# Routing of a mixture of experts moved from between the attention's units to behind its last one

## The chip, the cores and the metric

The kernel runs on one core of a Trainium2 chip. The metric is the device time of one execution in microseconds (us). The core has five engines with a queue each: TensorE (PE), VectorE (DVE), ScalarE (ACT), GpSimd (POOL) and SyncE (SP), which here only issues DMAs. Engines wait for each other by semaphores. A program part that is written as one block ends with a barrier of all five engines: none starts on the next block before each has come to the end of its own queue.

## The reference

`x` is 8 batches of 512 tokens with 128 channels. Four layers are added to it in turn, each on the layer-normalized input:

```
x = x + power_attention(layernorm(x))   # 16 heads of 8, (q.k)^2 with a decay
x = x + ffn(layernorm(x))               # 8 experts, top 1
x = x + delta_rule(layernorm(x))
x = x + ffn(layernorm(x))               # the same weights
```

The expert layer, which the change touches, is

```
logits = (x @ w_red) @ (wg / |wg|).T          # 8 experts
gates  = softmax(logits); idx = argmax(gates)
y      = gelu(x @ w1[idx] + b1[idx]) @ w2[idx] + b2[idx]
out    = y * gates[idx]
```

## The kernel before

The program is four blocks: `attention`, `experts` (f=0), `delta_rule`, `experts` (f=1).

**Attention.** A batch is 24 units (`NU`), each a strip of the causal score matrix. All loops are unrolled in Python, and each engine has its own function `batch(b, k)` that loops over units `n` and fixes the order of its queue by hand: numbers such as `TURN`, `QK`, `VALUES`, `SUMS`, `FIN` and the `R_...` constants say behind which unit a piece of other work stands. For a unit PE makes scores (`scores`, L1154) two units ahead, DVE takes their magnitude (`magnitude`, L795, one `a_mag` instruction a unit, also two ahead), ACT squares it (L552), POOL multiplies the diagonal blocks by a decay (`diagonal`, L415), and PE multiplies by the values (`attend`, L1183 and L1186) one unit later. Between them stands the preparation of the next batch: `a_xn` (L715) is DVE's behind unit 5 and `a_tail` (L773) behind unit 18, and POOL's `values_off` (L363) from unit 21 into unit 3 of the next batch. Behind units 2 and 20 the halves of a batch are finished (`turn_back` on PE, `finish` on DVE, `add_half` on POOL).

**Routing before.** While batch b runs, batch b-1 is routed for the first expert layer: `r_moments`, `r_deviation`, `r_normalize` on DVE, `r_turn` and `r_logits` on PE, `r_choose` on DVE, `r_ranks` on PE, `r_place` on DVE, all between units 8 and 19, and four `r_scatter` on POOL, each an indirect DMA of 128 rows of `r_xa` into `xs_dram`, at the expert's place that `r_place` found. In the last batch these stand two units earlier, with four more scatters. The gate's weights are made in batch 0 (`r_weights`, `r_gate`, `gate_turned`, `gate_weight`). Batch 7 alone is left to the `experts` block, which then makes the tables of tiles (`tables`), fills the expert areas' ends with blank rows (8 DMAs of `blank`, on ACT's queue) and loads on SP the weights and rows of the first slots.

**Experts.** 24 tiles of 256 rows go through slots of four: PE turns the rows (`turn_x`), multiplies by w1 (`up`, L1792) and w2 (`down`), turns back; POOL scatters the result. The order on PE is turn of the next slot, then `up` of this one. In the second `experts` block (f=1) all 8 batches are routed in five groups, `GROUPS` = (0), (1), (2,3), (4,5), (6,7).

Of the kernel before, what the change touches and what calls it, by code (L numbers as in the profile page):

```python
# [13 lines left out]
P = 128  # L14
# [24 lines left out]
ST = 256  # L39
# [7 lines left out]
SINGLE = tuple((b, b + 1) for b in range(B))  # L47
# [12 lines left out]
def attention(nc, x, xin, W, xs_dram, fs, keep, w_red, wg, b1, b2):  # L60
    with ExitStack() as ctx:
# [61 lines left out]
        r_stats = sb("r_stats", [P, TT, 6])  # L123
        r_mv = sb("r_mv", [P, TT, 2])
        r_rstd = sb("r_rstd", [P, 4, TT])
        r_xa = sb("r_xa", [P, 2, TT, C + 1])
        r_T = sb("r_T", [P, T])
        r_top = sb("r_top", [P, TT])
        r_hit = sb("r_hit", [P, TT, E])
        r_first = sb("r_first", [P, TT])  # L130
        r_oh = sb("r_oh", [P, TT, E], BF16)
        r_at = sb("r_at", [P, TT, E])
        r_pos_f = sb("r_pos_f", [P, TT])
        r_pos = sb("r_pos", [P, 2, TT], I32)
# [4 lines left out]
        b_in = sb("b_in", [E * NF + E, P])  # L139
        before, ones_r, one_row, pref, area = (keep[n] for n in ("before", "ones", "one_row", "pref", "area"))  # L140
        lgx, cnt, w_gate, blank = (keep[n] for n in ("lgx", "cnt", "w_gate", "blank"))
# [52 lines left out]
        def r_scat(c):  # L194
            return (fs["scat_done"], fs["scat_odd"])[c % 2]

        def r_logit_bank():
            return M1[:, 0:E * TT].rearrange("p (i e) -> p i e", e=E)

        def r_rank_bank(lo, hi):  # L200
            return M1[:, 64 + E * lo:64 + E * hi].rearrange("p (i e) -> p i e", e=E)
# [10 lines left out]
        def _(sp):  # L212
# [54 lines left out]
            for b in range(1, B - 2, 2):  # L267
                batch(b, 1)
                batch(b + 1, 0)

        @block.gpsimd
        def _(pool):
# [52 lines left out]
            def const(ins):  # L325
# [24 lines left out]
                      allow_small_or_imprecise_dtypes=True).then_inc(fs["f_consts"], 1)  # L350

# [66 lines left out]
            def r_index(c):  # L418

                if c >= 2:  # L420
                    pool.wait_ge(r_scat(c), 16 * TT * (c // 2))
                pool.iota(r_xa[:, c % 2, :, C], [[P, TT]], base=T * c, channel_multiplier=1,
                          allow_small_or_imprecise_dtypes=True).then_inc(fs["id_done"], 1)

            def r_scatter(c, i):
                pool.wait_ge(fs["pos_done"], c + 1)
                pool.wait_ge(fs["id_done"], c + 1)
                pool.indirect_dma_start(xs_dram[:, :], bass.IndirectOffsetOnAxis(ap=r_pos[:, c % 2, i:i + 1], axis=0),
                                        r_xa[:, c % 2, i, :], None).then_inc(r_scat(c), 16)
# [7 lines left out]
            def batch(b, k, first=False, last=False):  # L437
                for n in range(NU):
# [9 lines left out]
                    if n in R_SCATTER and b >= 2:  # L448
                        r_scatter(b - 2, R_SCATTER.index(n))
                    if n == R_SCALE2 + 1 and not first:  # L450
                        r_index(b - 1)
                    if last:
                        if n in R_SCATTER_LAST:
                            r_scatter(b - 1, R_SCATTER_LAST.index(n))
                        continue
# [17 lines left out]
        def _(act):  # L473
# [103 lines left out]
            def batch(b, k, first=False, last=False):  # L577
                for n in range(NU):
# [19 lines left out]
                    if last:  # L598
                        continue
# [2120 lines left out]
```

## Time and profile before

| | us |
|---|---|
| median of 3 runs | 1153.15 |
| lowest, highest | 1153.13, 1154.1 |
| the profiled execution | 1146.83 |
| its span, first to last instruction | 1145.0 |
| PE, DVE, ACT, POOL busy in it | 851.1, 760.2, 535.8, 562.0 |

The profiled execution was 6.3 us shorter than the median. Times in the rows count from the start of its span. Stretches are cut where the magnitude of a unit starts on DVE: 82.00 is unit 0 of batch 1 (`batch` starts anew with a 1024-column magnitude behind `a_rnorm`), 55.32 unit 8 of batch 0, 75.17 unit 20, and so on for the others.

### The profile page before, as it was taken

To read this page: it belongs to the slowest core of one execution; us is meant where nothing else is said; L and a number is where in the kernel's file an instruction comes from. 1 tells how busy PE (TensorE), PEld (TensorE's weight loads), DVE (VectorE), ACT (ScalarE), POOL (GpSimd) and SP (SyncE) were. 2 spreads that over 40 slices of the span, in tenths; PEclk is the share of its full clock that TensorE was granted. 3 is DMA by queue.
4 is the path that set the end of the run, shared out by engine and by line. 5 is a ranking of instruction groups with operands and counts; after the bars stand their busy time and mean duration, and the time that the engine had idled before them with its cause. 6 is when DMAs were issued, how large, how long until landed. Compare 5 with 4: busy or idle time off the path is not lost. (4 is left out here: it accounts for less than half of the span.)

```text
span 1145.0 us, 26725 instructions
## 1 busy us (share of the span) xinstructions
PE 851.1 (74%) x9326; PEld 632.7 (55%) x9326; DVE 760.2 (66%) x1722; ACT 535.8 (47%) x1219; POOL 562.0 (49%) x698
## 2 busy tenths in 40 slices
PE   3678888888888753999188999467867674629992
PEld 2455555555555542888124786156655563528881
DVE  7577687786877741223364889999999997512224
ACT  4577667586675721454055220255555531115450
POOL 4456557575665631445550010277777841533442
PEclk9998888797887965999688999878889886559996
DMA  5342241432414004566338400000020110155665
GB/s 162 112 157 91 68 159 41 134 98 70 159 41 134 9 14 139 168 202 187 100 58 109 74 1 0 0 1 0 0 73 0 37 38 7 40 157 163 196 195 165
DMA packets 129207, 101.80 MB, mean 89 GB/s; under 512 B 20640, under 2 KB 116832, under 8 KB 129056
## 3 DMA queue, kind: packets, MB, share of 16 engines
q1 hardware_dynamic: 120080, 87.27, 27.6%
q0 software_dynamic: 5120, 10.53, 2.6%
q10 hardware_dynamic: 3904, 2.61, 0.7%
q8 instruction: 68, 1.11, 0.4%
q14 instruction: 35, 0.29, 0.1%
HBM read 57.98 MB, written 35.45 MB: 82 GB/s over the span
## 5 line engine op out<-in xcount | busy, mean ns | idle before, releaser
L795 DVE TENSOR_SCALAR a_mag<-a_pS 128x1024 int32<-128x1024 int32 (+1 forms) x192 | 179.9, 949 | 66.6 <-PE a_pS L1154 65.7
L552 ACT ACTIVATE a_pw<-a_mag,a_eps_a 128x1024 f32<-128x1024 f32 (+1 forms) x192 | 175.0, 936 | 56.7 <-DVE a_mag L795 50.7
L1438 POOL DMA_INDIRECT ys_dram<-f_yo,f_who x96 | 92.1, 960 | 133.6 <-DVE f_yo L1703 116.9
L415 POOL TENSOR_TENSOR a_pw<-a_pw,a_decay 128x256 f32<-128x256 f32 x128 | 93.4, 730 | 105.2 <-ACT a_pw L552 104.5
L1154 PE MATMUL a_pS<-a_qf,a_kf 64*64 64x192 bf16 (+3 forms) x1536 | 112.2, 272 | 5.2 <-DVE a_mag L795 4.5
L1513 ACT ACTIVATE f_hs<-f_bH,f_bs 128x256 f32<-128x256 f32 x192 | 75.4, 475 | 69.0 <-PE f_bH L1792 69.0
L2613 PE MATMUL d_c<-d_pb_p,ident 128*128 128x256 f32 x256 | 72.3, 452 | 42.1 <-POOL d_pb_p L2096 42.1
L1186 PE MATMUL a_pOff<-a_pw,a_vo 128*18 128x64 f32 x3584 | 95.9, 241 | 1.2 <-issue 1.2
L1792 PE MATMUL f_bH<-f_xsT,f_w1s 128*128 128x256 f32 x384 | 95.6, 394 | 0.0
L1688 DVE TENSOR_SCALAR f_ysT<-f_bY,f_bs 128x256 f32<-128x256 f32 x48 | 23.2, 483 | 108.2 <-PE f_bY L1802 108.2
L1802 PE MATMUL f_bY<-f_hs,f_w2s 128*128 128x256 f32 x384 | 90.8, 379 | 0.0
L2613 PEld LDWEIGHTS d_c<-d_pb_p,ident 128*128 128x128 f32 x256 | 58.5, 232 | 56.3 <-issue 40.8
L1154 PEld LDWEIGHTS a_pS<-a_qf,a_kf 64*64 64x64 bf16 x1536 | 65.8, 116 | 30.7 <-DVE a_mag L795 7.6
L2613 PE MATMUL d_c<-d_pb_d,ident 128*128 128x256 f32 (+1 forms) x256 | 64.6, 419 | 21.7 <-POOL d_pb_d L2096 21.7
L2090 POOL TENSOR_TENSOR d_pb_p<-d_Q,d_s_sb 128x512 f32<-128x512 f32 x32 | 37.5, 1171 | 83.1 <-ACT d_s_sb L2198 83.1
L1186 PEld LDWEIGHTS a_pOff<-a_pw,a_vo 128*18 128x18 f32 x3584 | 68.6, 110 | 15.9 <-issue 11.4
L1792 PEld LDWEIGHTS f_bH<-f_xsT,f_w1s 128*128 128x128 f32 x384 | 72.4, 199 | 8.9
L1802 PEld LDWEIGHTS f_bY<-f_hs,f_w2s 128*128 128x128 f32 x384 | 69.4, 190 | 7.5
L2613 PEld LDWEIGHTS d_c<-d_pb_d,ident 128*128 128x128 f32 x256 | 53.1, 220 | 33.1 <-POOL d_pb_d L2096 24.6
L363 POOL TENSOR_TENSOR a_vo<-a_vd,a_reach 128x1008 f32<-128x1008 f32 (+6 forms) x56 | 66.0, 1194 | 1.1 <-issue 1.1
L1703 DVE COPY f_yo<-f_bO 128x256 f32<-128x256 f32 x48 | 20.4, 425 | 62.0 <-PE f_bO L1813 62.0
L2194 ACT ACTIVATE d_G<-d_c,d_g_ahead 128x64 f32<-128x64 f32 x64 | 24.1, 376 | 71.2 <-DVE d_og L2431 71.2
(395 smaller groups left out, 1837.9 us busy)
## 6 DMA issues: line engine op xcount, KB each, us to landing
parts_scratch<-a_parts SPq DMA_DIRECT2D x32, 384.0 KB, 3.4
f_w1s<-in_L_ffn_w_dram SPq DMA_DIRECT2D x48, 256.0 KB
f_w2s<-in_L_ffn_w_dram SPq DMA_DIRECT2D x48, 256.0 KB
a_kf<-parts_scratch SPq DMA_DIRECT2D x16, 512.0 KB, 4.8
a_qf<-parts_scratch SPq DMA_DIRECT2D x16, 512.0 KB, 5.6
f_xs<-xs_dram SPq DMA_DIRECT2D x48, 129.0 KB, 2.3
parts_scratch<-a_parts SPq DMA_DIRECT2D x16, 256.0 KB, 2.4
xs_dram<-blank ACTq DMA_DIRECT2D x16, 129.0 KB, 4.2
```

What stands on the lines that cost most here:

```text
L363: pool.tensor_tensor(vo[:, vo_at(j, j + 1):vo_at(j, j + 1) + n, :, :], vd[:, k, j, :, :].unsqueeze(1).broadcast_to([P, n, NP, 18]), reach[ ...
L415: pool.tensor_tensor(own, own, decay[:, k, m, hf:NP:2, :], ALU.mult)\
L552: act.activation(pw[:, n % 4, 0:N], mag[:, n % 3, 0:N], ACT.Square, bias=eps_a[:, 0:1])\
L795: dve.tensor_scalar(mag[:, n % 3, 0:2 * N].bitcast(I32).rearrange("p (l t) -> p l t", l=2), pS[:, 2 * (n % 2):2 * (n % 2) + 2, 0:N].bitcas ...
L1154: ins = pe.matmul(pS[lo:hi, 2 * (n % 2) + Q // 2, at:at + L * (end - first)], kf[lo:hi, k, p, L * m:L * m + L], qf[lo:hi, k, p, L * first: ...
L1186: ins = pe.matmul(pOff[lo:hi, L * i:L * i + L], vo[:, vo_at(m, i), p, :], wi, start=False, stop=(m == NM - 2), skip_group_check=True)
L1438: pool.indirect_dma_start(ys_dram[f][:, :], bass.IndirectOffsetOnAxis(ap=who[:, q, a:a + 1], axis=0), yo[:, q, a, :], None).then_inc(ys_ou ...
L1513: ins = act.activation(hs[:, q % 2, n, :], bH[:, 2 * (q % 2) + n // 2, ST * (n % 2):ST * (n % 2) + ST], ACT.Gelu, bias=bs[:, q, n:n + 1])
L1792: ins = pe.matmul(bH[:, 2 * (q % 2) + n // 2, ST * (n % 2):ST * (n % 2) + ST], w1s[:, q, P * n:P * n + P], xsT[:, q % 2, :], start=True, s ...
L1802: ins = pe.matmul(bY[:, 0:ST], w2s[:, q, n, :], hs[:, q % 2, n, :], start=(n == 0), stop=(n == NF - 1))
L2090: pool.tensor_tensor(po[:, 0:8], Q[:, :, :, bass.ds(c, 1)].rearrange("p k j c -> p k (j c)").unsqueeze(3) .broadcast_to([P, HD, CH, HD]), ...
L2613: ins = pe.matmul((c5, c6)[a][:, 0:64 * chunks].rearrange("p (c x) -> p c x", x=64), ident[:, :], po[:, k], start=(k == 0), stop=(k == 15))
```

## The change

The constants `R_...` of the single batches are gone. In batches 1 to 6 nothing is routed, and in batch 0 no gate weights are made. In the last batch, batch 0 and batch 1 are routed (`R_FIRST`), the gate's weights are made before them (`R_GATE`), and moments of batches 2 and 3 are taken (`R_NEXT`). Behind the last unit, still in the attention's block, the groups (2,3), (4,5) and (6,7) are routed, with the last batch's `dia_copy`, `finish` and `turn_back` between their steps, and then `tables` and `scores` follow. SP issues the 8 blank fills at the end of the same block. POOL issues 8 scatters in the last batch, 16 behind it, and the last 8 in the `experts` block. In both `experts` blocks SP now loads the weights of slot 0 alone ahead of its wait for the scatters and fills, and then rows and weights by turns. The second block's routing is as it was.

```diff
-        R_MOMENTS, R_DEVIATE, R_SCALE, R_SCALE2, R_TURN, R_LOGITS, R_CHOOSE, R_RANK, R_PLACE = 8, 10, 11, 13, 14, 16, 17, 18, 19
-        R_SOONER = 2
-        R_SCATTER = (5, 7, 13, 15)
-        R_SCATTER_LAST = (18, 19, 20, 21)
-        FIN = (20, 2)
+        FIN = (19, 2)
+        R_FIRST = {"moments": (1, 5), "deviate": (2, 6), "scale": (3, 7), "turn": (5, 9), "logits": (7, 11),
+                   "choose": (8, 12), "rank": (9, 13), "place": (10, 14)}
+        R_SCATTER = (12, 16)
+        R_GATE = {"turn": 3, "copy": 4, "weight": 5, "keep": 6}
+        R_NEXT = {"moments": (15, 17), "deviate": 18}
...
+            sp.wait_ge(fs["end_done"], 1)
+            for e in range(E):
+                row = sp.value_load(end_i[0:1, e:e + 1], min_val=e * AREA, max_val=e * AREA + B * T)
+                sp.dma_start(xs_dram[bass.ds(row, ST), :].rearrange("(p a) c -> p (a c)", p=P),
+                             blank[:, :, :].rearrange("p a c -> p (a c)")).then_inc(fs["fill_done"], 16)
...
             batch(B - 1, 1, last=True)
+            pool.wait_ge(fs["scat_first"], 16 * 2 * TT)
...
+            for g in (2, 3):
+                pool.wait_ge(fs["pos_done"], g + 1)
+                pool.wait_ge(fs["id_done"], g)
+                for b in range(*GROUPS[g]):
+                    for i in range(TT):
+                        r_scatter(b, i, "scat_done")
...
             batch(B - 1, 1, last=True)
+            r_deviation(2)
+            r_normalize(2, 2)
+            r_normalize(3, 2)
+            r_moments(4)
             dia_copy(B - 1, 1)
+            r_moments(5)
+            r_variance(3)
             for part in range(5):
                 finish(B - 1, 1, 1, part)
-            dve.wait_ge(s["fin_step"], 10 * B)
+            r_choose(2)
+            r_deviation(3)
+            r_normalize(4, 3)
+            r_place(2)
+            r_normalize(5, 3)
+            r_moments(6)
+            r_moments(7)
+            r_variance(4)
+            r_choose(3)
+            r_deviation(4)
+            r_normalize(6, 4)
+            r_place(3)
+            r_normalize(7, 4)
+            r_choose(4)
+            r_place(4)
+            tables()
+            scores()
...
             batch(B - 1, 1, last=True)
+            r_turn(2)
+            r_turn(3)
             attend(B - 1, 1, NU - 1)
+            r_logits(2, 2)
+            r_logits(3, 2)
             turn_back(B - 1, 1, last=True)
+            r_ranks(2)
+            for g in (3, 4):
+                for b in range(*GROUPS[g]):
+                    r_turn(b)
+                for b in range(*GROUPS[g]):
+                    r_logits(b, g)
+                r_ranks(g)
...
-            for q in range(SLOTS - 1):
-                weights(0, q, f > 0)
-            sp.wait_ge(s["scat_done"], 16 * TT * (B // 2 + 1) + 16 * NT * f)
-            sp.wait_ge(s["scat_odd"], 16 * TT * (B // 2 - 1))
+            sp.wait_ge(s["texp_done"], f + 1)
+            weights(0, 0, f > 0)
+            sp.wait_ge(s["scat_done"], 16 * (NT - 2 * TT) + 16 * NT * f)
+            sp.wait_ge(s["scat_first"], 16 * 2 * TT)
             sp.wait_ge(s["fill_done"], 16 * E * (f + 1))
...
-            for q in range(SLOTS - 1):
+            for q in range(SLOTS):
+                if q:
+                    weights(0, q, f > 0)
                 rows(0, q, f > 0)
-            weights(0, SLOTS - 1, f > 0)
-            rows(0, SLOTS - 1, f > 0)
```

DVE in batch 6, units 8 to 12. The names that begin with `a_r_` are the routing of batch 5. Before:

```order
L865 BN_STATS a_r_stats<-x 128x6 x4
L868 BN_AGGR a_r_mv<-a_r_stats 128x2 x4
L870 TENSOR_SCALAR a_r_rstd<-a_r_mv 128x4
L795 TENSOR_SCALAR a_mag<-a_pS 128x256
L795 TENSOR_SCALAR a_mag<-a_pS 128x1024
L732 COPY a_gates<-a_M 128x4x8 x2
L735 COPY a_gates<-a_M 128x64
L795 TENSOR_SCALAR a_mag<-a_pS 128x1024
L875 TENSOR_TENSOR a_r_rstd<-a_r_rstd 128x4
L877 TENSOR_TENSOR a_r_rstd<-a_r_rstd 128x4
L879 TENSOR_SCALAR a_r_rstd<-a_r_rstd 128x4
L882 TENSOR_TENSOR a_r_rstd<-a_r_rstd 128x4
```

After, the same units:

```order
L843 TENSOR_SCALAR a_mag<-a_pS 128x256
L843 TENSOR_SCALAR a_mag<-a_pS 128x1024
L780 COPY a_gates<-a_M 128x4x8 x2
L783 COPY a_gates<-a_M 128x64
L843 TENSOR_SCALAR a_mag<-a_pS 128x1024
L851 COPY a_dia_sb<-a_pDia 128x512
L843 TENSOR_SCALAR a_mag<-a_pS 128x1024
L843 TENSOR_SCALAR a_mag<-a_pS 128x768 x4
```

The moments and the deviation have left this place, and `dia_copy` follows the magnitudes alone.

PE from the last units of the attention to the block's end. `L1183` is `attend`, `L1208` the last `turn_back`. Before:

```order
L1183 MATMUL a_pDia<-a_pw,a_vd 18x64 [waits a_pdg_done]
L1183 MATMUL a_pDia<-a_pw,a_vd 18x64 x3
L1208 MATMUL a_M<-a_ident,a_off_sb 128x128 [waits a_fin_step,a_dia_done,a_off_done]
L1208 MATMUL a_M<-a_ident,a_off_sb 128x128 x3
L1208 MATMUL a_M<-a_ident,a_dia_sb 128x128 x4
L61 UNCONDITIONAL_BRANCH
L1720 UNCONDITIONAL_BRANCH [waits barrier_Pool_Activation_PE_DVE_SP_release]
L1727 MATMUL f_bB<-ident,f_xa 128x128 [waits f_rT_sb,f_xnf_done]
```

After, where `L1200` is `r_turn`, `L1304` `attend`, `L1213` `r_logits`, `L1328` `turn_back` and `L1228` the start of `r_ranks`:

```order
L1200 MATMUL a_pS<-a_ident,a_r_xa 128x128 [waits a_mag_done,f_xnf_done]
L1200 MATMUL a_pS<-a_ident,a_r_xa 128x128 x3
L1304 MATMUL a_pDia<-a_pw,a_vd 18x64 [waits a_pdg_done]
L1304 MATMUL a_pDia<-a_pw,a_vd 18x64 x3
L1213 MATMUL a_pS<-w_gate,a_rest 128x8 [waits f_rT_sb]
L1213 MATMUL a_pS<-w_gate,a_rest 128x8 x3
L1213 MATMUL a_pS<-w_gate,a_rest 128x8 [waits f_rT_sb]
L1213 MATMUL a_pS<-w_gate,a_rest 128x8 x3
L1328 MATMUL a_M<-a_ident,a_off_sb 128x128 [waits a_fin_step,a_dia_done,a_off_done]
L1328 MATMUL a_M<-a_ident,a_off_sb 128x128 x3
L1328 MATMUL a_M<-a_ident,a_dia_sb 128x128 x4
L1228 MATMUL a_pS<-first_cnt,one_row 128x72 [waits f_cnt_sb,f_oh_done]
```

Two batches' turns now stand ahead of the last `attend`, and their logits ahead of `turn_back`.

SP where the attention's block ends. Before:

```order
L61 UNCONDITIONAL_BRANCH
L1366 UNCONDITIONAL_BRANCH [waits barrier_Pool_Activation_PE_DVE_SP_release]
L1372 TENSOR_LOAD f_texp [waits f_texp_done]
L1372 ISA x2
L1375 ISA
L1375 DMA f_w1s<-in_L_ffn_w_dram 128x512
L1379 DMA f_w2s<-in_L_ffn_w_dram 128x4x128
L1381 ISA
L1381 DMA f_bs<-bT 128x5
```

After; `L294` and `L295` are the last of the eight blank fills, `L1509` and `L1513` the rows of slot 0:

```order
L295 ISA
L295 DMA xs_dram<-blank 128x258
L61 UNCONDITIONAL_BRANCH
L1491 UNCONDITIONAL_BRANCH [waits barrier_Pool_Activation_PE_DVE_SP_release]
L1495 TENSOR_LOAD first_texp [waits f_texp_done]
L1495 ISA x2
L1498 ISA
L1498 DMA f_w1s<-in_L_ffn_w_dram 128x512
L1502 DMA f_w2s<-in_L_ffn_w_dram 128x4x128
L1504 ISA
L1504 DMA f_bs<-bT 128x5
L1509 TENSOR_LOAD first_t_row [waits f_fill_done,f_zero_done,f_scat_first,f_scat_done]
```

The fills stand ahead of the barrier, and one slot's weights instead of three ahead of the rows.

## Rows read from the trace of the kernel before

**Rows 1.** The page's first line, which has the span.
```profile
span 1145.0 us, 26725 instructions
```

**Rows 2.** Timeline of DVE: start, length, then the instruction; last magnitude of the attention included.
```profile
82.00 1.23 DVE L795 TENSOR_SCALAR a_mag<-a_pS 128x1024 int32<-128x1024 int32 x1 [0.18 <-PE a_pS L1154]
...
180.47 1.23 DVE L795 TENSOR_SCALAR a_mag<-a_pS 128x1024 int32<-128x1024 int32 x1 [1.29 <-PE a_pS L1154]
...
371.56 1.23 DVE L795 TENSOR_SCALAR a_mag<-a_pS 128x1024 int32<-128x1024 int32 x1 [1.29 <-PE a_pS L1154]
...
412.02 0.41 DVE L795 TENSOR_SCALAR a_mag<-a_pS 128x256 int32<-128x256 int32 x1
```

**Rows 3.** Stretches: length, busy time (count) of each engine, granted clock, DMA share, GB/s.
```profile
55.32:75.17 19.85, 16.19 (x443) 11.36 (x441) 14.59 (x28) 15.07 (x24) 10.01 (x16) 1.00 0.63 213
75.17:82.00 6.83, 4.92 (x139) 3.80 (x140) 5.62 (x13) 3.67 (x5) 3.31 (x4) 1.00 0.15 36
82.00:99.69 17.69, 15.14 (x287) 9.85 (x286) 11.19 (x17) 12.94 (x20) 13.66 (x17) 0.81 0.01 2
195.18:219.34 24.16, 19.05 (x451) 14.12 (x450) 19.08 (x46) 16.10 (x27) 13.67 (x20) 0.86 0.54 185
219.34:228.22 8.88, 7.44 (x144) 5.55 (x145) 5.99 (x14) 3.62 (x5) 4.77 (x6) 0.62 0.11 24
228.22:242.93 14.71, 13.25 (x288) 8.03 (x287) 11.60 (x17) 13.12 (x20) 12.77 (x16) 1.00 0.03 8
```

**Rows 4.** Groups of DVE instructions from 180.47 to 371.56 us: busy us, mean ns.
```profile
L889 DVE TENSOR_SCALAR a_r_xa<-x,a_r_mv,a_r_rstd 128x128 f32<-128x128 f32 x16 | 5.6, 391 | 0.1
...
L877 DVE TENSOR_TENSOR a_r_rstd<-a_r_rstd 128x4 f32<-128x4 f32 x4 | 0.6, 162 | 0.1
```

**Rows 5.** Timeline of PE at the start of batch 1, with what released it.
```profile
87.05 0.31 PE L1183 MATMUL a_pDia<-a_pw,a_vd 128*18 128x64 f32 x8 [1.57 <-POOL a_pw L415]
```

**Rows 6.** The same stretches' view, for the first part of the last batch.
```profile
371.56:384.14 12.58, 11.12 (x288) 7.05 (x291) 9.63 (x12) 11.47 (x17) 10.88 (x13) 1.00 0.01 3
384.14:407.78 23.64, 18.47 (x419) 13.39 (x417) 17.35 (x38) 13.12 (x19) 10.93 (x15) 0.74 0.05 13
```

**Rows 7.** Timeline between attention and first expert stage, engine by engine.
```profile
422.14 0.42 DVE L830 TENSOR_TENSOR x<-x,a_y 128x256 f32<-128x256 f32 x1
...
433.21 0.17 DVE L1599 CAST f_pos<-f_pos_f 128x4 int32<-128x4 f32 x1
...
434.87 8.13 ACTq L1496 DMA_DIRECT2D xs_dram<-blank  x8
...
438.15 0.96 POOL L1430 DMA_INDIRECT xs_dram<-f_xa,f_pos  x1 [0.30 <-issue]
...
438.10 0.39 SPq L1375 DMA_DIRECT2D f_w1s<-in_L_ffn_w_dram  x1
...
440.57 0.36 SPq L1375 DMA_DIRECT2D f_w1s<-in_L_ffn_w_dram  x1
...
448.06 3.07 SPq L1390 DMA_DIRECT2D f_xs<-xs_dram  x3
...
452.13 3.62 PE L1792 MATMUL f_bH<-f_xsT,f_w1s 128*128 128x256 f32 x8
```

**Rows 8.** Timeline of the second expert stage's routing, which already has groups of two batches.
```profile
992.64 0.22 DVE L1584 TENSOR_TENSOR f_oh<-pref,f_first 128x64 bf16<-128x64 f32 x1
...
996.00 2.14 DVE L1565 TENSOR_SCALAR f_xa<-x,f_mv,f_rstd 128x128 f32<-128x128 f32 x8
...
999.10 3.51 PE L1738 MATMUL f_bH<-w_gate,f_rT 128*128 128x8 f32 x16
...
1003.68 0.23 DVE L1584 TENSOR_TENSOR f_oh<-pref,f_first 128x64 bf16<-128x64 f32 x1
...
1005.63 0.17 DVE L1599 CAST f_pos<-f_pos_f 128x8 int32<-128x8 f32 x1
...
1014.94 0.96 POOL L1430 DMA_INDIRECT xs_dram<-f_xa,f_pos  x1 [0.30 <-issue]
```

More of the change, by code:

```diff
@@ L46 @@
 GROUPS = ((0, 1), (1, 2), (2, 4), (4, 6), (6, B))
-SINGLE = tuple((b, b + 1) for b in range(B))
+NG = len(GROUPS)
 AREA = B * T + ST
@@ L57, with attention @@
 EPS_K = 1e-12
-def attention(nc, x, xin, W, xs_dram, fs, keep, w_red, wg, b1, b2):
+def attention(nc, x, xin, W, xs_dram, fs, keep, first, w_red, wg, b1, b2):
     with ExitStack() as ctx:
@@ L139, in attention @@
         b_in = sb("b_in", [E * NF + E, P])
+        end_f = sb("end_f", [P, E])
+        end_i = sb("end_i", [P, E], I32)
+        num = sb("num", [P, E])
+        more = sb("more", [P, E, NT * P // ST])
+        n_til = sb("n_til", [P, E])
+        ends = sb("ends", [P, E])
+        past = sb("past", [P, NS, E])
+        gone = sb("gone", [P, NS, E])
+        texp_f = sb("texp_f", [P, NS])
+        done = sb("done", [P, NS])
+        lsum = sb("lsum", [P, NT])
         before, ones_r, one_row, pref, area = (keep[n] for n in ("before", "ones", "one_row", "pref", "area"))
-        lgx, cnt, w_gate, blank = (keep[n] for n in ("lgx", "cnt", "w_gate", "blank"))
+        lgx, cnt, pos, last_xa, texp, t_row = (first[n] for n in ("lgx", "cnt", "pos", "last_xa", "texp", "t_row"))
+        w_gate, blank, tile_at, k_at, one8, score = (keep[n] for n in ("w_gate", "blank", "tile_at", "k_at", "one8", "score"))
         pS = psum("pS", [P, 4, T])
@@ new lines, in r_ranks @@
+                seen = (cnt[0:1, (g - 1) % 2, :] if g else area[0:1, :]).unsqueeze(1).broadcast_to([1, n + 1, E])
+                pe.matmul(r_ranks_in(g, 0, n + 1), one_row[0:1, :], seen, start=True, stop=False, skip_group_check=True)
+                pe.matmul(r_ranks_in(g, 0, n), before[:, :], r_oh[:, lo:lo + n, :], start=False, stop=False,
+                          skip_group_check=True)
+                for i in range(n):
+                    ins = pe.matmul(r_ranks_in(g, i + 1, n + 1), ones_r[:, :],
+                                    r_oh[:, lo + i:lo + i + 1, :].broadcast_to([P, n - i, E]), start=False,
+                                    stop=(i == n - 1), skip_group_check=True)
@@ L1636, in scores @@
                 dve.wait_ge(s["lg_exp"], 3 * f + 3)
-            if f == 0:
-                moments(B - 1)
-                variance(NG - 1)
-                deviation(NG - 1)
-                normalize(NG - 1)
-                choose(NG - 1)
-                place(NG - 1)
-            else:
+            if f == 1:
                 moments(0)
@@ L2687, in build @@
             "score": sb("score", [P, NT]),
-            "lgx": sb("lgx", [P, NT, E]),
-            "cnt": sb("cnt", [P, 2, E]),
-        }
-        attention(nc, x, xin, W, xs_dram, s, keep, w_red, wg, b1, b2)
-        experts(nc, x, xs_dram, ys_dram, s, keep, 0, w_red, wg, w1, b1, w2, b2, out)
+        }
+        with ExitStack() as both:
+            first = {n: both.enter_context(nc.sbuf_tensor("first_" + n, shape, dt)) for n, shape, dt in (
+                ("lgx", [P, NT, E], F32), ("cnt", [P, 2, E], F32), ("pos", [P, NT], I32), ("texp", [P, NS], I32),
+                ("t_row", [P, NS], I32), ("last_xa", [P, 2, TT, C + 1], F32))}
+            attention(nc, x, xin, W, xs_dram, s, keep, first, w_red, wg, b1, b2)
+            experts(nc, x, xs_dram, ys_dram, s, keep, first, 0, w_red, wg, w1, b1, w2, b2, out)
         counted = ((s["fw_in"], 64), (s["zero_done"], 16 * IDLE // ST), (s["wgT_ps"], 2), (s["wgT_sb"], 5),
```

507 lines of the change are left out of this document (275 added, 232 removed).

## Prediction

> **What bounds the kernel now.** I read the span [rows 1], and then the attention as stretches between magnitudes on DVE, since that instruction is the beat of the loop [rows 2]. Batches 1 to 6 take 371.56 - 82.00 = 289.56 us, and the last one from its first magnitude to its last 412.02 - 371.56 = 40.46. Batch 3 stands for the six: its period is 24.16 + 8.88 + 14.71 = 47.75 us, with the units 8 to 19 (routing between them), 20 to 23, and 0 to 7 of the next batch [rows 3]. In no stretch is an engine full. PE is nearest (19.05 of 24.16, 13.25 of 14.71), DVE has 19.08 of 24.16. So the period is set by a ring: PE's scores wait for the scores' buffer, which DVE's magnitude frees, and so every instruction that DVE does between two magnitudes, and every matmul between two units on PE, is paid in part. Batch 0 is the comparison that the trace holds: the same twelve units with no earlier batch to route, only the gate's small copies, take 19.85 us and units 20 to 23 take 6.83, at a granted clock of 1.00 (2.4 GHz), where batch 3 has 24.16 at 0.86 and 8.88 at 0.62 [rows 3]. DVE's busy time is 19.08 in the one and 14.59 in the other. Between attention and experts the profile shows another regime, a chain of latencies with all engines mostly idle: 412.02 last magnitude, 422.14 last addition to x, 433.21 places of the last batch, scatters until 438.15 + 0.96, weights and rows on SP, and the first `up` at 452.13 [rows 7]. That is 40.1 us from last magnitude to first `up`.
>
> **Batches 1 to 6 lose their routing.** DVE's share of it is 24.2 us in four batches, in 16 groups of which the costliest and the last are shown [rows 4], so 6.05 a batch, for PE some turns and logits, for POOL four scatters of 0.96 that start 1.27 apart when they run back to back (as [rows 8]). I take the new period from stretches, not from this sum. Middle: 19.85, as in batch 0. Units 20 to 23: 6.83. Front: here two rows differ, 14.71 at 1.00 (batch 3 into 4) and 17.69 at 0.81 (batch 0 into 1) [rows 3]. In the longer one POOL has the most to do for its length, 13.66, and PE waits 1.57 us for POOL's diagonal blocks [rows 5], since `values_off` stands in front of them. A faster middle and end bring PE to this place sooner while POOL's work there has stayed, so I take the front that follows a fast end, 17.69. The period is 19.85 + 6.83 + 17.69 = 44.37, less 0.3 for the gate copies that batch 0 still had: 44.1. Six of them are 264.6, **24.9 us less**; batch 0 loses its copies, another 0.3. Bounds: with 14.71 for the front the period is 41.4 and the gain 41.2; with a middle in which only the DVE wait shrinks, by 1.8 a batch, it is 10.8.
>
> The clock is part of this. The rows have 0.86 and 0.62 where routing stood and 1.00 where it did not [rows 3], but also 0.81 in a front without any, so the change need not give every stretch the fast level.
>
> **The last batch gets two batches to route.** Its first part before is 12.58, 2.13 less than the 14.71 of a usual one, because no next batch is prepared [rows 6]. The fast predecessor makes the usual one 17.69, so 15.6 without that preparation. Into it now come moments, deviation, scaling and the choice of batch 0 and part of batch 1, about 7.5 us of DVE (6.05 for one batch, and the first steps of the other), where DVE has 12.58 - 9.63 = 3.0 idle in the short version and 6 in the long: I put 3 on the path, 18.6. The middle holds the rest and the moments of batches 2 and 3 instead of one batch and four more scatters; I leave it at 24 (23.64 now), and the end to the last magnitude at 4.24 (412.02 - 371.56 - 12.58 - 23.64). Together 46.8 against 40.46: **6.3 us more**. Bounds: 2 (front 12.58 and the three us of overlap taken half) to 11 (all 7.5 exposed).
>
> **Behind the last unit six batches' worth of tail.** I count on the old clock from 412.02. PE now does the turns of batches 2 and 3 ahead of the last `attend` and their logits ahead of `turn_back`; 16 logits took 3.51 where they stand in f=1 [rows 8], of which DVE's own steps hide about one, so `finish` ends at 425.1 and not 422.56 (422.14 + 0.42). The one-hot of group 2 follows 1.3 later, 426.4. From there three groups of two batches are chained as in f=1: one-hot to one-hot 1003.68 - 992.64 = 11.04, one-hot to places 1.95 [rows 8]. I take 10.0 a cycle, 11.04 less half of the 2.14 of normalizing [rows 8], since half a group's is done earlier. One-hots at 426.4, 436.4, 446.4, the last places at 448.3, against 433.4 before. SP's eight fills wait for the ends that come with them: from 449.8 for 8.13, as the same eight took on ACT's queue [rows 7], until 457.9. They stood behind the barrier before, beside the weights' DMAs; now they stand in front of it, and the whole core waits for SP. Barrier at 458.5. Only then can POOL issue the last 8 scatters: 459.0, and 7 x 1.27 + 0.96 further 468.9 (before, 4 of them ended at 439.1). The 16 scatters ahead of the barrier take 20.3 us from 428.4 on and are hidden behind DVE's chain and the fills until 448.7; they would show if the chain were 10 us shorter. With 2 us for the landing SP issues the rows of slot 0 at 471.2, against 448.06. Slot 1's rows then wait for slot 1's weights, 2.47 (440.57 - 438.10), and 1.02 for the rows themselves, so they go at 474.7 and not 1.02 behind the first. PE turns slot 1 ahead of `up` of slot 0, and that `up` came 3.05 behind the issue of slot 1's rows (452.13 - 449.08) [rows 7]: 477.7, **25.6 us more** than 452.13. Bounds: 20, with cycles of 9 and a `finish` that nothing delays; 30, with cycles of 11.04 and fills of 1.2 each behind a busy queue.
>
> On this place a rule of the Trainium skill speaks against the change. Rows first: in f=1 scatters start 1.27 apart, 0.96 busy and 0.30 issue, though DVE works through the next group's choice beside them [rows 8]. "SBUF — State Buffer", section "SBUF: two separate sides", says that descriptors of a DMA from GpSimd can't be written while VectorE holds the port that both share, and gives some 620 ns alone against some 3100 ns beside a copy. By that figure, an estimate from the page, the 16 scatters would last 16 x (3.1 + 0.3) = 54 us, until 482, and the change would be some 24 us slower still. By that rule rows 8 should show it, and they do not: the trace disagrees. The sum goes without it.
>
> **Second expert stage.** Its SP order changes too: slot 1's rows go 2.4 us later, but fills and rows meet fewer weight DMAs. I take **+0.7**, bounds -2 and +2.5.
>
> **Sum.** -25.2 + 6.3 + 25.6 + 0.7 = +7.4. The profiled execution, 1146.83, becomes 1154.2; the median of the runs, which is 6.3 above it, 1153.15 + 7.4 = **1160.5**.
>
> **Rivals.** First, faster: the fronts stay at 14.71 and the clock at 1.00 through the whole attention, since POOL too has lost four scatters a batch. For it: batch 3 into 4 has it, and DVE and PE lose work in every batch. Against it: the only front behind an undisturbed end is the 17.69 one. It gives -41.2 - 0.3 + 6.3 + 25.6 + 0.7 = -8.9, **1144**; if the last batch is cheap as well, 1141. Second, no change: a period of 42.9, which saves 32.2 in six batches, or a tail of 18 instead of 25.6 with all else as said, **1153**. The forecast turns at that period, only 1.2 us under 44.1, which is why I don't give slower more. Third, slower by far: the middles do not fall to batch 0's, because its sums and copies follow other inputs and PE's low clock returns (0.62 to 0.86 now [rows 3]); at a period of 46 the six batches give 13.6 and not 24.9, so +18.7, **1172**. Fourth, the change does not hide what it queues: POOL's 16 scatters beside DVE's three groups keep no pace of 1.27 but wait for each of its steps, at worst two and a half times as long, 3.2 each, so that they end at 479.6 instead of 448.7; then barrier, last scatters and rows come 21.1 later, **1182**. Against it stand the 0.96 and 0.30 of rows 8, in the same company. That the change doesn't do what it says, so that the units lose their routing and keep their period, because a wait between PE and POOL sets it, is the far end of the third.
>
> **How the numbers follow.** Forecast (1156 to 1168) 0.56, first rival 0.20, second 0.14, third 0.08, fourth 0.02. About 2.3 us, 0.2%, is what a measurement of this kernel can tell from no change. Faster 0.21 is the first rival and one in a hundred from beside it, same 0.14 the second, slower 0.65 the rest. The range leaves out the far half of the first rival, part of the third and the fourth: 1146 to 1170.
>
> **What would show it.** In the profile after: magnitudes of unit 0 in batches 1 to 7 lie 44.1 apart, with clock 1.00 in the middles and PE released by POOL in the fronts (41.4 and no such release would make the first rival right). The last batch takes 47 from first to last magnitude. The fills on SP end just ahead of the barrier, eight scatters follow it, and the first `up` comes 65 to 66 us behind the last magnitude, against 40.1. The second expert stage starts its first `up` within 1 us of before, counted from its routing. I am wrong if DVE's chain of three groups runs well under 10 us a cycle, if the fills are not on the way to the barrier, or if the periods miss 44.1 by more than 1.

## The result and the profile after

| | before | after |
|---|---|---|
| median us | 1153.62 (4 runs) | 1166.73 (4 runs) |
| lowest, highest | 1153.13, 1154.95 | 1163.71, 1170.0 |
| ratio | | 1.0112, 95% interval 1.0095 to 1.0129 |

The changed kernel is 13.1 us slower; 7.4 were forecast (1160.5), and the time lies inside the range of 1156 to 1168. The execution that was traced is the slowest of the four, 1170.0, with a span of 1168.2. Medians and ratios leave out one slow execution of the changed kernel, 1380.69 us at a mean clock of 0.586, among those measured again below.

Timeline of DVE, the beats that stand beside [rows 2]: start, length, instruction.

```profile
81.50 1.22 DVE L843 TENSOR_SCALAR a_mag<-a_pS 128x1024 int32<-128x1024 int32 x1 [0.27 <-PE a_pS L1275]
...
337.31 1.23 DVE L843 TENSOR_SCALAR a_mag<-a_pS 128x1024 int32<-128x1024 int32 x1 [0.27 <-PE a_pS L1275]
...
391.18 0.36 DVE L843 TENSOR_SCALAR a_mag<-a_pS 128x256 int32<-128x256 int32 x1
```

Batches 1 to 6 take 255.81 us (289.56 before), the last one 53.87 (40.46). Stretches of batch 4 (front, middle, end), then of the last batch, with length, busy PE, PEld, DVE, ACT, POOL, clock, DMA share and GB/s as in [rows 3, 6]:

```profile
211.10:227.88 16.78, 14.40 (x287) 8.64 (x288) 11.18 (x16) 12.69 (x20) 14.48 (x17) 0.90 0.01 3
227.88:247.21 19.33, 15.84 (x464) 11.30 (x462) 14.11 (x25) 14.65 (x23) 9.49 (x15) 1.00 0.64 206
247.21:253.17 5.96, 4.20 (x112) 3.07 (x112) 5.37 (x11) 4.16 (x5) 2.93 (x5) 1.00 0.30 81
```

```profile
337.31:358.08 20.77, 14.87 (x297) 9.62 (x301) 15.23 (x42) 13.07 (x23) 14.08 (x17) 0.87 0.01 2
358.08:387.05 28.97, 23.23 (x461) 16.76 (x460) 19.07 (x55) 12.20 (x16) 13.48 (x17) 0.68 0.05 16
```

The tail, engine by engine, answers to [rows 7]. `L960` is the one-hot of a group, `L949` the first step of a choice, `L974` the places.

```profile
404.79 0.42 DVE L878 TENSOR_TENSOR x<-x,a_y 128x256 f32<-128x256 f32 x1
...
406.15 0.22 DVE L960 TENSOR_TENSOR a_r_oh<-pref,a_r_first 128x64 bf16<-128x64 f32 x1
...
415.31 0.23 DVE L960 TENSOR_TENSOR a_r_oh<-pref,a_r_first 128x64 bf16<-128x64 f32 x1
...
419.32 0.23 DVE L970 TENSOR_TENSOR a_r_at<-a_pS,a_r_oh 128x64 f32<-128x64 f32 x1 [1.91 <-remote]
...
427.61 0.22 DVE L949 TENSOR_REDUCE a_r_top<-a_pS 128x8 f32<-128x64 f32 x1 [6.34 <-remote]
...
432.44 0.17 DVE L974 CAST first_pos<-a_r_pos_f 128x8 int32<-128x8 f32 x1
...
433.90 8.43 SPq L295 DMA_DIRECT2D xs_dram<-blank  x8
...
443.46 0.96 POOL L1552 DMA_INDIRECT xs_dram<-first_last_xa,first_pos  x1 [13.38 <-POOLq L61]
...
452.30 0.95 POOL L1552 DMA_INDIRECT xs_dram<-first_last_xa,first_pos  x1 [0.30 <-issue]
...
455.31 0.40 SPq L1513 DMA_DIRECT2D f_xs<-xs_dram  x1
...
458.72 0.39 SPq L1513 DMA_DIRECT2D f_xs<-xs_dram  x1
...
461.37 3.62 PE L1901 MATMUL f_bH<-f_xsT,f_w1s 128*128 128x256 f32 x8
```

From last magnitude to first `up` it is 461.37 - 391.18 = 70.2 us, against 40.1. So at the first `up` the balance is -0.5 - 33.7 + 13.4 + 30.1 = +9.3 (9.24 by the two starts of the first `up`). The two traces differ by 23.2 at the end, however, and of the other 14 the forecast had only its 0.7 for the second stage. They are in the tiles of both expert stages and in the opening of the second. Stretches of the kernel before (tiles of the first stage, delta rule, opening of the second, its tiles), and then of the changed one:

```profile
452.13:543.84 91.71, 91.36 (x454) 78.57 (x454) 24.75 (x87) 44.84 (x115) 39.90 (x42) 0.97 0.64 182
543.84:952.87 409.03, 302.18 (x1187) 217.09 (x1185) 345.73 (x591) 159.53 (x540) 188.01 (x220) 0.86 0.17 34
952.87:1025.61 72.74, 28.68 (x151) 24.70 (x149) 37.37 (x199) 10.08 (x22) 31.09 (x33) 0.52 0.24 71
1025.61:1117.76 92.15, 91.78 (x454) 78.41 (x454) 24.76 (x87) 44.84 (x115) 39.89 (x42) 0.97 0.63 180
```

```profile
461.37:557.97 96.60, 92.74 (x454) 77.75 (x454) 25.16 (x87) 44.73 (x115) 39.78 (x42) 0.98 0.63 177
557.97:966.46 408.49, 302.92 (x1187) 219.25 (x1185) 346.68 (x598) 159.25 (x540) 187.46 (x220) 0.86 0.18 34
966.46:1043.60 77.14, 28.85 (x149) 24.75 (x149) 36.48 (x193) 10.07 (x22) 30.98 (x33) 0.52 0.21 59
1043.60:1141.91 98.31, 94.74 (x454) 77.60 (x454) 24.86 (x87) 44.72 (x115) 40.20 (x42) 0.97 0.63 176
```

The tiles, the opening and the second tiles grow by 4.9, 4.4 and 6.2 us; the delta rule and the end of the program give 1.5 back. The first theory for this was SP's new order, which gives up a head start of three slots of weights.

### The profile page after: what moved, and what is told of

Same layout as the page of the kernel before. It is cut to its first block and busy times, and to the rows that moved or that the text cites. A ratio compares the mean times of both kernels' runs of the same rounds, so it can differ in the third digit from the quotient of the medians.

```text
span 1168.2 us, 26609 instructions
## 1 busy us (share of the span) xinstructions
PE 848.9 (73%) x9317; PEld 624.2 (53%) x9317; DVE 747.1 (64%) x1683; ACT 533.3 (46%) x1210; POOL 558.5 (48%) x693
## 5 line engine op out<-in xcount | busy, mean ns | idle before, releaser
L1275 PE MATMUL a_pS<-a_qf,a_kf 64*64 64x192 bf16 (+3 forms) x1536 | 109.4, 267 | 18.0 <-DVE a_mag L843 15.8
L1802 DVE TENSOR_SCALAR f_ysT<-f_bY,f_bs 128x256 f32<-128x256 f32 x48 | 23.2, 484 | 117.9 <-PE f_bY L1911 97.1
L1307 PE MATMUL a_pOff<-a_pw,a_vo 128*18 128x64 f32 x3584 | 91.9, 232 | 0.9 <-issue 0.9
L1307 PEld LDWEIGHTS a_pOff<-a_pw,a_vo 128*18 128x18 f32 x3584 | 65.0, 104 | 16.5 <-issue 12.0
L1891 PE MATMUL f_bA<-ident,f_xs 128*128 128x128 f32 x96 | 21.2, 306 | 58.4 <-DMA f_xs<-xs_dram 39.3
```

The costliest lines, as they stand in the source:

```text
L1275: ins = pe.matmul(pS[lo:hi, 2 * (n % 2) + Q // 2, at:at + L * (end - first)], kf[lo:hi, k, p, L * m:L * m + L], qf[lo:hi, k, p, L * first: ...
L1307: ins = pe.matmul(pOff[lo:hi, L * i:L * i + L], vo[:, vo_at(m, i), p, :], wi, start=False, stop=(m == NM - 2), skip_group_check=True)
```

## Is it SP's order, or the first trace?

The control and the first three edits ran on one chip, with the kernel before at 1153.82.

> The changed kernel as it is, as the measure for its neighbours. Theory S (the second reading of the traces: SP's new order takes the head start that three slots of weights gave, and costs 4.9 us in the first stage's tiles, 6.2 in the second's and about 1 at each start): ratio to before 1.011, PE's waits for f_xs in the tiles again some 4 us a stage, last up behind first up 96 to 98 us instead of 92. Rival J (the execution that was profiled was a disturbed one, 1170.0 against 1163.7 for the lowest): the same stretches come out at 92 this time. The second stage's routing, 13.6 us from one-hot of group 2 to that of group 3 instead of 10.95, should be back at 11 by both, since the code is the same.

Measured: ratio 1.0129 (1.0099 to 1.0158), the time within the noise of the first result. Tiles 96.7 and 95.4, opening 76.6, tail 70.35.

```diff
-            weights(0, 0, f > 0)
+            for q in range(SLOTS - 1):
+                weights(0, q, f > 0)
```

> One part undone: SP loads the weights of three slots ahead of its wait for scatters and fills, and then three rows, in both expert stages, as before. Theory S: first to last up 92 us in both stages (96.6 and 98.3 now), first up of the first stage 2 to 3 us later than now, that of the second 1 earlier, together 8 to 10 us less than the changed kernel run beside it. Rival J: no gain in the tiles, 2 us more in the first stage, so 0 to 2 us slower than the changed kernel.

Measured: ratio 1.0107 (1.008 to 1.0135), tiles 95.6 and 95.9, opening 77.2. Theory S falls: with the head start back the tiles are still 3.9 and 3.7 us over those of the first trace. The ratios of the two runs do not differ beyond their intervals. The first `up` did not come later either, 68.2 behind the last magnitude instead of 70.2: slot 1's weights no longer stand between the rows of slots 0 and 1.

Two runs of the kernel before followed, one as it is and one with the new order alone.

> The kernel before, unchanged, for a second trace of it: the first was of an execution of 1146.83, 6.3 below the median of its runs. Theory P (the first trace is not typical of the tile stages): first to last up 95 to 97 us in both stages, as in all four traces of the changed order and in the one with SP's old order, and 75 to 77 us from the delta rule's end to the first up of the second stage; batches 1 to 6 289 to 291. Theory L (something in the changed program other than SP's order makes the second stage slower): 92, 92 and 72.7 again.

Stretches of that second trace of the kernel before, at the same places (first tiles, opening, second tiles):

```profile
451.59:546.14 94.55, 91.78 (x454) 77.02 (x454) 24.75 (x87) 44.84 (x115) 39.93 (x42) 0.99 0.63 176
...
954.98:1029.85 74.87, 28.85 (x150) 24.77 (x149) 36.49 (x193) 10.08 (x22) 31.17 (x33) 0.52 0.24 69
1029.85:1126.13 96.28, 93.69 (x454) 77.60 (x454) 24.77 (x87) 44.84 (x115) 39.92 (x42) 0.98 0.60 173
```

Theory P holds in the main: 2.8, 2.1 and 4.1 of the 4.9, 4.4 and 6.2 us were luck of the first traced execution (span 1145.0, here 1152.6), while the first `up` comes within 0.6 us of it (batches 1 to 6 289.99, tail 39.6). Leaving the first trace out, the first tiles take 93.4 to 97.5 us and the second ones 95.2 to 98.3 in all traces of either kernel, so the 2 us that are left in each lie within the scatter. The single batches repeat less well than their sum: 51.08, 44.45, 51.12 and three of 47.8 here, 47.42, 51.05 and four of 47.8 in the first trace.

```diff
-            for q in range(SLOTS - 1):
-                weights(0, q, f > 0)
+            weights(0, 0, f > 0)
```

> The kernel before with the new order on SP alone, in both expert stages: one slot's weights ahead of the wait, then rows and weights by turns. If the order costs what the first two traces suggested, 10 us slower than before (ratio 1.009); if, as the run with the old order in the changed kernel says, the order moves the first up earlier by 1 to 3 us in the first stage and gives 1 back in the tiles, within 3 us of before (0.998 to 1.003).

Measured: ratio 1.0012 (1.0000 to 1.0024), so the order costs 0 to 2.8 us. First `up` at 39.6 behind the last magnitude, as without it; tiles 96.7 and 95.2.

## The one number that the prediction passed over

```diff
-        FIN = (19, 2)
+        FIN = (20, 2)
```

> The changed kernel with FIN = (20, 2), so that the first half of each batch is finished behind unit 20 and not 19, the one part of the change that the prediction took for nothing. If it is nothing: batches 1 to 6 together 252 to 262 us as in the five traces of the changed order, median within 3 us of the changed kernel (1166 to 1171). If the earlier place gives the 1.5 us a batch by which the periods beat the forecast (42.6 against 44.1): 9 us slower.

Measured: 1174.12, ratio 1.0165 (1.0146 to 1.0183), and batches 1 to 6 in 265.16 us (346.50 - 81.34), against 252.0 to 263.4 in the nine traces with 19 there (mean 256.7). Stretches of its batch 4:

```profile
215.06:233.88 18.82, 15.32 (x287) 10.02 (x288) 11.14 (x18) 12.93 (x20) 14.79 (x17) 0.82 0.01 3
233.88:253.85 19.97, 16.80 (x448) 11.95 (x450) 14.14 (x25) 14.64 (x23) 9.53 (x15) 0.91 0.64 212
253.85:259.52 5.67, 4.54 (x136) 3.28 (x131) 5.35 (x11) 4.05 (x5) 2.61 (x5) 1.00 0.18 40
```

Middle and end lie within 0.7 us of the changed kernel's (19.33 and 5.96) and lean opposite ways; the front is 18.82 and not 16.78. The next front of each trace shows where the time goes. Its 104 matmuls from the magnitude of unit 3 to that of unit 5 (columns as before), in the changed kernel and then with 20:

```profile
261.23:264.72 3.49, 3.31 (x104) 2.68 (x108) 2.82 (x5) 3.49 (x5) 3.47 (x5) 1.00 0.00 0
```

```profile
267.82:273.74 5.92, 5.74 (x104) 4.54 (x108) 2.82 (x5) 3.66 (x5) 4.48 (x6) 0.52 0.01 3
```

From the magnitude of unit 20 to that of unit 8 the kernel with 20 takes 24.45 us and the changed one 22.07, and these two units, at the half clock (1.2 GHz) in the one and the full in the other, are the whole difference. POOL's later values for the next batch come at the same distance from unit 20 in both (the second ones start 9.4 or 9.5 us behind it, the third 11.8), so it is not they that make the difference. What 19 moves is `add_half`, from behind POOL's first product of values to ahead of it, and with it PE's waits for POOL's diagonal blocks: 2.22 us in one piece, 1 us before the clock falls, with 20, and 1.35 and 0.82 with 19. That this is what keeps the clock up is argued and not shown. Five of the six fronts with 20 have over 4 us of half clock between the magnitudes of units 2 and 5, and seven of the 54 in the nine traces with 19.

So the 8.5 us go with the clock. By the time of the whole the place is worth 4 to 6 us (1.0165 against 1.0129 and 1.0112). The sum of 264.6 lies 0.6 us from this kernel's, but by terms that cancel: fronts 18.5 in the mean for 17.69, ends 5.70 for 6.83, middles 19.96 for 19.85.

> The kernel before with FIN = (19, 2), the one small part of the change alone. If the earlier first half pays by itself, as it did without the routing (1.6 us a batch): batches 1 to 6 280 us instead of 290, median 1144. If it pays only where the front of a batch is the long kind, which the kernel before has in its first batch alone (units 3 and 4 at 2.29 and 3.67): within 2 us of before, and slower by some if unit 19, which already holds the places of the routed batch, gets the finish as well.

Measured: 1169.58, ratio 1.0138 (1.0115 to 1.0161). The second case, but far worse than "slower by some". Stretches of batch 4 in the kernel before with 19:

```profile
235.62:251.20 15.58, 13.13 (x288) 7.90 (x287) 11.60 (x17) 13.33 (x20) 14.80 (x18) 1.00 0.02 7
251.20:274.78 23.58, 18.05 (x451) 13.38 (x450) 19.06 (x47) 16.19 (x27) 13.62 (x20) 0.93 0.56 189
274.78:284.07 9.29, 7.16 (x144) 5.42 (x145) 6.05 (x14) 3.61 (x5) 2.29 (x4) 0.63 0.11 24
```

Batches 1 to 6 take 298.07, 8 us more (and batch 0 3 us more): unit 19 holds the places of the routed batch as well, and in batch 4 the magnitude of unit 22 comes 4.59 us behind that of unit 21. In the traces of batches 1 to 6 the same number is worth 8 us less without routing in the units, and costs 8 more with it.

## Where the tail spends 70 us

```diff
+            pool.wait_ge(fs["pos_done"], NG)
+            for i in range(2 * TT):
+                r_scatter(6 + i // TT, i % TT, "scat_done")
```

The same eight scatters leave the `experts` block.

> The last eight scatters are issued in the attention's block, ahead of its barrier, and not behind it; nothing else. Theory T (the tail is a row of things that could lie side by side: eight fills of 8.4 us on SP, then the barrier, then eight scatters of 10.1 us on POOL): both run side by side from 433 on, the rows of slot 0 go at about 446.5 instead of 455.3, the first up some 9 us earlier, the whole 8 to 9 us shorter than the changed kernel. Rival F (fills and scatters write the same memory and slow each other, or the rows wait for the landing of the fills anyway): under 4 us gained.

Measured: 1165.13, ratio 1.0085 (1.0058 to 1.0112) where the unchanged one beside it had 1.0129 (1.0099 to 1.0158). These intervals overlap, so the tail has to tell: 64.0 us from last magnitude to first `up`, 6.4 less. Two thirds of theory T's 9 us came, and the rest met the next wait:

```profile
434.11 9.44 SPq L295 DMA_DIRECT2D xs_dram<-blank  x8
446.72 0.37 SPq L1501 DMA_DIRECT2D f_w1s<-in_L_ffn_w_dram  x1
```

Beside the scatters the fills take 9.4 instead of 8.4, the first weights go 3.2 us behind the last fill instead of 1.3, and the weights of slot 0, which were hidden under the scatters, now stand alone ahead of the rows.

The split of the fills puts `range(E // 2)` on SP and the rest behind ACT's last instruction in the block.

> Four of the eight blank fills are issued by ACT and four by SP, both ahead of the barrier. Theory T: the barrier comes 4 us earlier (fills end at 438 to 439 instead of 442.3), and as the last eight scatters wait for it, first up and end come 4 us earlier. Rival F (it is the write to memory and not the issue of 1.05 us each that takes the 8.4 us): barrier where it was, within 1 us of the changed kernel.

Measured in the trace: fills from 428.33 on, over by 432.1, the first of the last eight scatters 47.7 us behind the last magnitude instead of 52.3, first `up` 65.9 instead of 70.3, as theory T has it, 4.4 less. Two queues at once take 3.7 and 3.8 us for four fills each, so the issue takes the time, about 0.93 each here, and not the memory:

```profile
428.33 3.72 SPq L295 DMA_DIRECT2D xs_dram<-blank  x4
...
433.24 0.95 POOL L1557 DMA_INDIRECT xs_dram<-first_last_xa,first_pos  x1 [8.74 <-POOLq L61]
```

The time of the whole does not tell it: 1168.59, ratio 1.0142 (1.0098 to 1.0186), its runs between 1158.05 and 1173.13. The part up to the last magnitude, the same code in all of these kernels, spreads by 11 us between traces (batches 1 to 6 from 252.0 to 263.4), more than the edit is worth. The traced execution here is the fastest of its four.

That spread goes with the clock. Batches 1 to 6 in the shortest (`e1_sp_old`) and the longest (`e11_hold`) of the nine traces with 19:

```profile
81.25:333.27 252.02, 207.69 (x5172) 139.23 (x5172) 182.90 (x290) 190.04 (x282) 161.67 (x211) 0.95 0.34 108
```

```profile
81.56:344.93 263.37, 216.99 (x5172) 146.78 (x5172) 182.52 (x290) 190.36 (x282) 161.67 (x211) 0.91 0.33 103
```

The work is the same, and PE is busy 9.3 us longer in the 11.4 us by which they differ. The seven others lie between (0.93 to 0.95 for 254.4 to 255.8 us, 0.92 for 258.5 and 261.5), and the kernel with 20 continues the row with 0.89 for 265.16.

The remaining question was the third cycle of DVE's chain: one-hot to one-hot 9.16 us (415.31 - 406.15) and then 13.3 (428.64 - 415.31), with handovers that start 2 us late: `L970` and `L949` in the rows above, released by nothing that the trace shows ("remote"). It is the same to 0.1 us in the six traces in which only other places were edited. PE's counts of group 3 and ACT's copy of them, then DVE's one-hot of group 4:

```profile
416.27 0.45 PE L1232 MATMUL a_pS<-a_r_oh,ones 128*128 128x64 bf16 x8
419.05 0.18 ACT L602 ACTIVATE first_cnt<-a_pS 128x8 f32<-128x8 f32 x1 [6.40 <-remote]
...
428.64 0.22 DVE L960 TENSOR_TENSOR a_r_oh<-pref,a_r_first 128x64 bf16<-128x64 f32 x1
```

The copy starts 2.33 us behind the end of PE's counts.

```diff
+            pool.wait_ge(fs["pos_done"], NG)
             for g in (2, 3):
-                pool.wait_ge(fs["pos_done"], g + 1)
```

> The changed kernel with POOL's sixteen scatters of batches 2 to 5 held back until the last places are there, so that nothing is scattered while DVE, PE and ACT route the last groups. In the changed kernel the third cycle of that chain is 13.4 us from one-hot to one-hot, the second 9.1, and three handovers in it start some 2 us behind what they waited for. Theory Q (the scatters that run beside them delay the handovers between engines): one-hots at 15.0, 24.1 and 33 to 34 us behind the last magnitude instead of 37.5, the last places at 36 instead of 41.3. Theory N (something else, code or plain order): 37.5 and 41.3 again. By both the scatters then end some 25 us later than now: first up 13 to 19 us later, whole 1180 to 1186.

The same counts and copy in that run, and then DVE; its last magnitude stands at 397.29:

```profile
422.36 0.45 PE L1232 MATMUL a_pS<-a_r_oh,ones 128*128 128x64 bf16 x8
422.85 0.18 ACT L602 ACTIVATE first_cnt<-a_pS 128x8 f32<-128x8 f32 x1 [4.11 <-PE a_pS L1232]
```

```profile
421.40 0.22 DVE L960 TENSOR_TENSOR a_r_oh<-pref,a_r_first 128x64 bf16<-128x64 f32 x1
...
429.49 0.23 DVE L949 TENSOR_REDUCE a_r_top<-a_pS 128x8 f32<-128x64 f32 x1 [4.42 <-PE a_pS L1213]
430.52 0.22 DVE L960 TENSOR_TENSOR a_r_oh<-pref,a_r_first 128x64 bf16<-128x64 f32 x1
...
432.48 0.17 DVE L974 CAST first_pos<-a_r_pos_f 128x8 int32<-128x8 f32 x1
```

The third cycle is 9.12 us like the second, the places are there 35.2 us behind the last magnitude instead of 41.3, and no handover is late. Theory Q holds: POOL's scatters beside the chain cost it 6.1 us, 4.2 in the third cycle and 1.9 between the last one-hot and its places. Two things narrow it. The scatters run beside the second cycle too, from 17.9 us behind the last magnitude on, and it takes 9.16 us as without them; the first late handover ends at 27.9. And the step that is late is each time one that waits for PE: `L602` and `L597` on ACT, `L949` and `L970` on DVE, 1.9 to 2.6 us behind the end of PE's work, while PE starts 0.05 us behind what it awaits from DVE, as without the scatters. What in the scatters does it (the writing of descriptors, the transfers, the semaphores), and why not from the first on, stays open. The run as a whole was 1178.4, ratio 1.0184, its first `up` 76.8 behind the last magnitude and not 13 to 19 later than 70.2: the expectation added the held scatters in full and forgot that the fills and the earlier places overlap with them.

## Why the last batch grew by 13 us

What PE and DVE waited for in the last batch of the changed kernel (us in total, times, longest):

```profile
PE a_M L1228 <- DVE a_r_oh L960: 3.6, 2, 3.1
PE a_M L1191 <- DVE bT L903: 2.6, 1, 2.6
...
PE a_M L1200 <- DVE a_r_xa L942: 1.3, 1, 1.3
...
DVE a_mag L843 <- PE a_pS L1275: 9.9, 7, 3.2
```

PE stands in its own queue for a one-hot or a copy of DVE, the next scores stand behind that, and DVE then waits for the scores.

> The moments and the deviation of batches 2 and 3 leave the last batch's units and stand behind its last unit; all else as in the changed kernel. If DVE's work between units is paid in full in this crowded batch: last batch 2.5 to 4 us shorter (50.3 to 53.9 in five traces), the tail from the last magnitude to the first up 2.5 to 4 longer, sum unchanged. If units hide it: last batch the same and the tail 3 longer. If it costs more than its own time between units (waits of PE and ACT behind it): last batch over 5 shorter.

Measured: 1170.26, ratio 1.0138 (1.0112 to 1.0163); last batch 55.15, tail 69.9. None of the three cases: 2.4 us of DVE's work left the last batch and it did not get shorter, and the tail that took it in did not get longer. For the tail this says that it had room. For the last batch it says little: the granted clock was 0.66 over it in this trace, the lowest of all, where the changed kernel had 0.78.

The next run spreads the same steps over more units (`rank` from (9, 13) to (11, 16), `place` from (10, 14) to (12, 17), the scatters from (12, 16) to (14, 19), and the rest likewise).

> The changed kernel with another table for the last batch: the same steps of the same two batches, but one unit more between what hands over from DVE to PE and back (ranks two units behind the choice instead of one, places with them, batch 1's logits to places two to three units later, gate's weights spread from unit 2 to 6). Theory H (the last batch is long because PE stands in its own queue for DVE's copy, one-hots and rows, 2.6, 3.6 and 1.3 us in the trace, and DVE then waits 9.9 us for scores): last batch 47 to 50 us instead of 50.3 to 55.2 in six traces, median 3 to 5 us below the changed kernel. Rival W (it is the amount of work and the half clock): last batch unchanged within 1 us of 53.

Measured: 1170.27, ratio 1.0142; last batch 52.96, as rival W says, and 74.1 in the tail. PE's waits for one-hot and copy are gone from the list, and others have come, 3.7 us for POOL's diagonal blocks and 3.0 for magnitudes. The same table in the next kernel had 49.45. So theory H is not shown. The last batch was 49 to 55 us in ten traces, by table and by execution alike, and it too goes with the granted clock: 49.45 us at 0.86, 55.15 at 0.66, and the eight others, 50.3 to 54.1, at 0.77 to 0.81. How much of the 13 us the clock has (0.78 over the batch, 0.83 before) and how much the added steps stays open. So does a third candidate, POOL's eight scatters, which this batch had before too, but spread over 29 us and now over 16: in the trace of the changed kernel the magnitude at 385.18 starts 1.4 us behind the end of its scores (383.77), with scatters beside it, and no run took them away. The tail got 3.9 us longer: its first one-hot came 1.4 later and its third cycle took 17.5 us instead of 13.3, with more late handovers in it. Why more is not shown.

> The changed kernel with all that its runs point to: four of the last eight scatters ahead of the barrier and four behind it, fills issued by SP and ACT by halves, SP's old order, the last batch's table spread. By the single runs the tail from last magnitude to first up shrinks from 70.2 to about 61 (9 from barrier and scatters: barrier 4 us earlier and four scatters less behind it, 5), the last batch by 3 to 5, the tiles by 1: 13 to 15 us below the changed kernel, so 1152 to 1156, level with the kernel before. If the parts overlap (SP's three weights then end the opening), 1157 to 1160.

Measured: 1162.43, ratio 1.0081 (1.0061 to 1.0101). Last batch 49.45, tail 65.8, tiles 93.4 and 96.9, in the fastest of its six executions (1154.78). The median is above both cases and 8 us above the kernel before. No version was found that beats the latter.

## The prediction, step by step

- **Batches 1 to 6: -24.9 forecast, -33.7 in the trace of the changed kernel (-26.2 to -37.5 over the nine).** The middle, 19.85 forecast and 20.1 in the mean, came as said. The step that failed is the choice of the long front, 17.69, against 16.6 measured, together with the end cut from the same rows, 6.83 against 5.97: some 6.6 and 5.2 us of the gain that it missed, from which the middle and the 0.3 a batch for the gate copies take 3 back. The pair holds for `FIN` at 20, and the list of parts left the move to 19 uncosted. The prediction had the wrong reason for the long front, too: it put it down to POOL's `values_off`, but the row carries a clock of 0.81, and where the clock does not fall the same work is 2.4 us shorter, though POOL's later values come no sooner. By its own sign, a period that misses 44.1 by more than 1, this step was wrong: the mean was 42.6.
- **Last batch: +6.3 forecast, +13.4 measured.** Front 18.6 forecast, 20.8 measured; middle 24 forecast, 29.0 measured. The sum counted DVE's time against DVE's idle time, and left the middle as it was because "the same amount" of routing stood there. What it left out, the steps that change engine inside one unit, the clock (0.68 in the middle, 0.74 before) and the scatters beside it, the runs do not separate; the cause of this term stays open.
- **Tail: +25.6 forecast, +30.1 measured.** The chain of causes is in the order that was said. Taken from 412.02, the fills were forecast from 37.8 on and came at 42.7; from there the forecast's 27.9 us to the first `up` stand against 27.5. The missing term is the 6.1 us that the scatters take from the chain beside them. Cycles of 10.0 us, where an undisturbed one takes 9.1, gave about one of these back. The scatters themselves were as fast as forecast, 0.96 each and 1.26 apart within a group. They were "hidden" in their own time and not in that of their neighbours. The prediction had weighed the opposite, scatters slowed by VectorE, and set it aside rightly.
- **Second stage: +0.7 forecast.** Against the second trace of the kernel before it is +2.3 in the opening and +2.0 in its tiles, +2.0 in those of the first stage. The tiles lie within their scatter (95.4 for the second ones when the changed kernel was measured again), and SP's order accounts for 0 to 2.8, by its own run.
- **Rivals.** The first one asked for fronts of 14.71 and a period of 41.4; single batches had 41.4 (batch 5), the mean was 42.6, below the 42.9 at which the forecast was to turn. Had the last batch and the tail cost what was forecast, the first `up` would have stood 2.3 us before that of the kernel before. Two errors of 9 and 11.6 us cancelled. That the median fell inside the range is owed to this, and is luck.
- **Where the range was built on one trace.** The 11.04 us of [rows 8] are a cycle of that chain without late handovers: in the second trace of the kernel before the cycle ahead of it took 12.87 us, with 4.03 us of "remote" wait ahead of `L1573`, where the first trace had 10.95.

## What to carry to other kernels

Cost every line of a table that moves, also the one that looks like a tidy-up: here, in the traces, one unit's shift of one step was worth 8 us with one sign in one surrounding and 8 with the other in the other. Read the clock of a row before its length is used as a price: the same 104 matmuls took 3.5 us or 5.9. When work is gathered behind a loop, sum the chain of handovers and not the busy time, and ask of each "hidden" stream of DMAs what it does to the engines beside it. Take two traces of a kernel before its small rows are used as prices, and settle edits of less than the scatter by stretches of the trace that the rest cannot disturb.

## What the runs showed of the hardware

- Handovers from PE to ACT and DVE came 1.9 to 2.6 us late, several in a row, while GpSimd issued indirect DMAs back to back: 13.3 us for a cycle that takes 9.1 with the scatters held back. Handovers from DVE to PE in the same cycle were not late, and the cycle before it was not either, though five of the scatters had been issued in it.
- The same attention code took 252.0 to 263.4 us for six batches from one execution to the next, at a granted clock of 0.95 in the shortest and 0.91 in the longest, with periods of 41.4 and 44.5 side by side in one trace. The kernel before took 289.6 to 290.0 in three traces (one of them with SP's new order), at 0.85 in each, though its single batches took 44.5 to 51.1.
- From the magnitude of unit 3 to that of unit 5, 104 matmuls took 3.49 us at a granted clock of 1.00 and 5.92 at 0.52.
